# Unread products of constants in TensorE's waits: a two-layer attention and mixture-of-experts kernel

## The reference, cut to what matters

```
x = x + attn0(layernorm(x), ctx)   # 16 heads of 16, in windows of 128 queries and 128 keys
x = x + moe0(layernorm(x))         # 16 experts, top 2 (sigmoid gates), and a shared expert of 512
x = x + attn1(layernorm(x), ctx)   # 16 heads; 256 tokens share 256 keys
x = x + moe1(layernorm(x))         # 8 experts of 1024, top 2 (softmax gates), with biases
```

## Time and profile before

| | |
|---|---|
| median of three runs | 954.8 us (952.94 to 958.06) |
| the profiled execution | 952.44 us |
| its span, first to last instruction | 950.5 us |
| TensorE busy | 793.5 us, 83% |
| VectorE, ScalarE, GpSimd busy | 610.0, 382.6, 235.5 us |
| mean granted TensorE clock | 0.904 of 2.4 GHz |

### The profile page before, as it was taken

The page is one execution under the profiler, slowest core; times in us unless marked ns, Lnnn a source line. Parts: engine busy times, 40 slices in busy tenths (PEclk is TensorE's granted clock), DMA queues, the critical chain, the costliest instruction groups (busy, mean ns, idle before and its releaser), DMA issues.

```text
span 950.5 us, 23219 instructions
## 1 busy us (share of the span) xinstructions
PE 793.5 (83%) x8478; PEld 596.2 (63%) x8479; DVE 610.0 (64%) x1397; ACT 382.6 (40%) x750; POOL 235.5 (25%) x203
## 2 busy tenths in 40 slices
PE   5988997897897999987869999874029999999993
PEld 3545564654556888864525666563019999999992
DVE  3546777466745766759565888676975665556561
ACT  3425556342322322222324556655324444444440
POOL 1100000100014777742100000020033544444431
PEclk9986999798999999998976999875559999999996
DMA  9966402244324333339625320167332333333334
GB/s 267 103 75 92 140 7 68 89 133 133 102 65 143 103 99 105 99 114 186 74 38 75 71 91 3 46 231 284 110 122 47 72 71 71 73 67 67 72 65 111
DMA packets 72973, 94.66 MB, mean 100 GB/s; under 512 B 14320, under 2 KB 58224, under 8 KB 72880
## 3 DMA queue, kind: packets, MB, share of 16 engines
q1 hardware_dynamic: 57088, 62.17, 27.6%
q0 software_dynamic: 13872, 29.24, 12.4%
q10 hardware_dynamic: 1952, 2.39, 0.7%
HBM read 63.09 MB, written 19.92 MB: 87 GB/s over the span
## 4 chain that ended last, share of the span: by engine, by line
PE 60%; DVE 16%; issue 6%; DMA 4%; ACT 3%; POOL 1%; POOLq 0%; DVEq 0%; SPq 0%; ACTq 0%
PE bank L879 16%; PE bank L892 13%; PE bank L672 5%; PE bank L693 4%; PE bank L798 3%; DVE arena L1606 3%; PE bank L641 3%; PE bank L864 2%; PE bank L749 2%; DVE neg_max L1316 2%; PE bank L659 2%; PE bank L787 2%; PE bank L790 2%; PE bank L687 1%; DMA sum_d<-arena,put_i 1%
## 5 line engine op out<-in xcount | busy, mean ns | idle before, releaser
L879 PE MATMUL bank<-arena 128*128 128x128 f16 x3024 | 303.8, 221 | 14.5 <-DVE arena L1611 12.5
L892 PE MATMUL bank<-arena 128*128 x1224 | 282.9, 275 | 4.7 <-DVE arena L1619 2.9
L879 PEld LDWEIGHTS bank<-arena 128*128 x3024 | 264.7, 99 | 31.5 <-issue 15.4
L1760 POOL DMA_INDIRECT arena<-xn_d,get_i x87 | 92.1, 1059 | 210.7 <-DVE arena L1606 100.1
L1184 ACT ACTIVATE arena<-bank,arena 128x128 f32<-128x128 f32 x312 | 86.4, 376 | 125.7 <-DMA arena<-in_exp_b 67.3
L1316 DVE TENSOR_REDUCE neg_max<-bank 128x2 f32<-128x512 f32 (+1 forms) x180 | 117.3, 684 | 28.7 <-PE bank L641 27.8
L892 PEld LDWEIGHTS bank<-arena 128*128 128x128 f16 x1224 | 120.2, 98 | 15.9 <-issue 13.1
L1056 ACT ACTIVATE arena<-bank 128x1024 f32<-128x1024 f32 x96 | 96.5, 1026 | 15.4 <-PE bank L659 15.0
L1770 POOL DMA_INDIRECT sum_d<-arena,put_i x39 | 63.3, 1622 | 111.9 <-DVE arena L1632 101.5
L1619 DVE TENSOR_TENSOR arena<-arena 128x512 f16<-128x512 f32 (+1 forms) x126 | 74.7, 593 | 4.3
L1744 POOL DMA_DIRECT2D xn_d<-arena x8 | 6.7, 840 | 276.4 <-DVE arena L1385 276.4
(11 more groups left out here) (185 smaller groups left out, 1129.4 us busy)
## 6 DMA issues: line engine op xcount, KB each, us to landing
arena<-arena SPq DMA_DIRECT2D x96, 128.0 KB, 5.2
arena<-in_exp_up SPq DMA_DIRECT2D x16, 512.0 KB, 3.7
arena<-in_exp_dn SPq DMA_DIRECT2D x6, 1024.0 KB, 6.4
arena<-in_exp_up SPq DMA_DIRECT2D x5, 1024.0 KB, 6.0
arena<-in_exp_b SPq DMA_DIRECT2D x39, 128.0 KB, 3.0
arena<-in_ctxT SPq DMA_DIRECT2D x8, 512.0 KB, 7.2
arena<-in_exp_dn SPq DMA_DIRECT2D x16, 256.0 KB, 4.0
xn_d<-arena POOLq DMA_DIRECT2D x8, 512.0 KB, 5.8
```

What stands on the lines that cost most here:

```text
L879: last = mm(upP[u][:, m // (UB // 2), m % (UB // 2) * P:(m % (UB // 2) + 1) * P], weights(e, 0, w, k * UPW[l] + m * P, P), rowsT[u][x][:, ...
L892: last = mm(yP[u], hidT[u][x][:, k], weights(e, 1, w, k * D, D), start=n == 0, stop=n == n_second - 1)
L1760: pool.indirect_dma_start(rows[i % 2], None, xn_d[l], bass.IndirectOffsetOnAxis(ap=get_i[:, i:i + 1], axis=0)).then_inc(s["rows_in"][i % 2 ...
```

## The change

A helper `keep_running(to, n, cols)` multiplies the identity with the first `cols` columns of `consts`, n times, in float32, into a stretch of PSUM that nobody reads. It is called in TensorE's program alone; no other engine's program changes. Four of its places also get a wait of their own, so that the PSUM stretch is free. The diff (context cut):

```
+        spare = bank[:, 4]
...
+            def keep_running(to, n, cols):
+
+                for _ in range(n):
+                    mm(to[:, 0:cols], ident, consts[:, 0:cols], start=True, stop=True)
...
                 def turn_tokens(c, u):
+                    if l == 0 and c == NC - 1:
+                        pe.wait_ge(s["xT_ready"], c)
+                        keep_running(trT[:, 0], 3, 3 * P)
                     pe.wait_ge(s["xn_ready"], c + 1)
...  first_maxima:
                 for m in range(lo, hi):
+                    if l and m >= 2:
+                        if m == 2:
+                            pe.wait_ge(s["v_ready"], NC)
+                        keep_running(spare, 5 if m == 2 else 1, 3 * P if m == 2 else P)
                     after(pe, s["max_read"], m - 1)
...  turn_first:
+                if l:
+                    keep_running(spare, 2, P)
                 pe.wait_ge(s["max_read"], 4 * KV[l])
...  attend, maxima:
                     for m in range(lo, hi):
+                        if isinstance(i, int) and i == 1:
+                            if l == 0 and m == 0:
+                                pe.wait_ge(s["v_ready"], NC)
+                            if l == 0 and m == 2:
+                                keep_running(spare, 5, 3 * P)
+                            elif m:
+                                keep_running(spare, 1, P)
                         after(pe, s["max_read"], i * NM + m - 1)
...  attend, step:
                             maxima(i + 2, SPREAD[l][p], SPREAD[l][p + 1])
+                        if p == 0 and isinstance(i, int) and 13 <= i < 13 + (1 if l else FIRST0):
+                            keep_running(spare, 2, 2 * P)
                         if p == 0 and not first:
                             turn_back(i - 1)
...  route:
                 def score(c, u):
+                    if l:
+                        keep_running(bank[:, 2], 2, 2 * P)
                     pe.wait_ge(s["xT_ready"], NC + c + 1)
...  invert:
+                if l:
+                    pe.wait_ge(s["routed"], 3)
+                    keep_running(bank[:, 2], 13, 3 * P)
                 pe.wait_ge(s["routed"], 4)
...
                 if l:
+                    keep_running(bank[:, 2], 6, 3 * P)
                     pe.wait_ge(s["routed"], 6)
...  experts:
+                if l:
+                    pe.wait_ge(s["w_lo"], PIECES - 1)
+                    keep_running(bank[:, 0], 4, 3 * P)
                 pe.wait_ge(s["w_lo"], PIECES)
                 may_multiply(0)
```

## The result

The changed kernel takes 951.88 us (median of 20 runs, 944.8 to 956.03), the kernel before, run beside it, 957.51 us (20 runs, 948.52 to 962.95). The ratio is 0.9943, with a 95% interval of 0.992 to 0.9967: faster by 5.6 us, where 12.8 were forecast (954.8 to 942). The direction is right and the size is not; the time lies just outside the range of 934 to 951. Of the 9.9 us between forecast and result, 2.7 belong to the kernel before, whose median was 954.8 us over the three runs shown and is 957.5 over twenty; the gain is 5.6 us for 12.8 all the same.

The account below looks back on a forecast made before the run. It took TensorE's granted clock to set much of the time, where the others wait for TensorE. Terms summed to -11.5 us: 940.9 on the profiled execution's scale, 942 us after adding half of 2.4; range 934 to 951.

Parts of the forecast that it names:

- T1: End of layer 0's projections: three products hidden in a 2.27 us wait hold the clock; -1.7 us (bounds 0 and -1.9).
- T4: Late attention steps: two products hold the clock in layer 1's step 13, -2.8 us; layer 0's two such places 0.
- T3: Layer 1's first attention steps: +0.25 us if the clock is lost, -6.7 if held; taken as -0.7.
- I add half: Last adjustment: the shown runs' median is 2.4 us above the profiled execution; half added for clock luck, 940.9 to 942 us.
- T2: Layer 0's first attention steps: five hidden products, but the clock falls in the unfilled second wait; -0.3 us (-3.2 if held).
- rival A: Clock holds through both attentions' second waits, so their first steps gain more: 933 us, chance 0.12.
- T5: Layer 1's route: products ahead of each chunk's scores hold the clock, half the time with a fall; -5 us (bounds -6.7, +1.2).
- Rival B: Clock falls in layer 1's route as before, since 8-column scores and transposes do not hold it: 948 us, chance 0.16.
- T6: Ahead of the placing's products in layer 1: 13 products (about 11 us) and six (3.9 us) stay hidden; 0 us.
- Rival D: Slower: unread products run at half clock and outlast their waits, at the placing above all; 962 us, chance 0.05.
- T7: Layer 1's first expert products: four products bring the clock back earlier; -1.0 us (bounds +0.7 and -1.4).

Follow-up runs that it names:

- attn_only: Kernel before plus only the unread products where both attentions begin (blocks of five, singles, two ahead of the transposed maxima): 985.56 us, ratio 1.0008.
- route_only: Kernel before plus only the two unread products ahead of each chunk's scores in layer 1's route: 979.16 us, ratio 0.9929.
- tr_route: Kernel before plus eight float32 transposes of the identity ahead of each chunk's scores in layer 1's route: 979.22 us, a single execution.
- second_wait: no_single plus three float32 products of 384 columns inside step 0 of both layers: 970.2 us, ratio 0.9838.
- held: f16_single plus float16 products of 384 columns inside step 0 of both layers (four, then seven): 965.28 us, ratio 0.9833.
- no_single: Changed kernel without the single products between the maxima, blocks of five kept: 967.96 us, ratio 0.9827; run again 975.87 us, ratio 0.9872.
- f16_single: Changed kernel with each single float32 product between the maxima replaced by one float16 product of 512 columns: 974.63 us, ratio 0.9917.
- no_attn: Changed kernel without any unread products where the attentions begin, the others kept: 976.57 us, ratio 0.9929.
- before_again: Kernel before, unchanged, run for a second profile: 990.21 us, mean clock 0.898.

## Why the prediction was right or wrong

**The failed steps: what each term is measured against, and the price of a single product.** The terms were differences to one execution, in which the clock fell at every place that has a term. Such falls are not in every execution. Step 13 of layer 1 took 9.2 us without any product in attn_only and route_only, and 10.7 in tr_route; the end of layer 0's projections was 12.6 us without products in route_only and tr_route (which are the kernel before up to the route), and 14.2 or 14.3 in the other three. On the mean over the five profiles without products, T1 is -1.0 and not -1.7, and T4 -1.4 and not -2.8: 2.1 us of the sum of 11.5. T3, below, had a price wrong and is +0.5 for -0.7: 1.2 more. On the other side, the route's products hold the clock throughout in five of ten profiles that have them (15.7 us); in two it fell and came back (16.9), in three it fell and stayed (20.1, 20.4 and 20.3 us).

The runs on record say the same of the clock without a profile. In 63 executions of the kernel before, in the three groups, the mean clock lies between 0.896 and 0.918, 0.907 on the average, and an execution with 0.001 more is about 0.6 us shorter. The profiled one had 0.904, which is 2 us of lost clock above the ordinary. It was 5 us below the median of its 20 runs all the same (952.44 for 957.51), and that of the changed kernel 3 below its own. "I add half" made the forecast gain 12.8 against the median, 1.3 more than the sum; no run shows a reason for it.

**T1**, right in its mechanism: the three products took 2.10 us at 45.86, the real ones followed with 0.33 to spare, PEclk was 1.00. -1.7 in this profile.

**T2**, right against rival A, +0.4 for -0.3 in size. The clock fell at 72.7 (73 to 76 was said) and stayed low to 86.3. That the unfilled second wait is the reason was an argument; second_wait and held show it: with products in it, and nothing else new in layer 0 against no_single and f16_single, its steps 0 and 1 take 10.5 and 10.3 us for 13.6 to 14.0.

**T3**, wrong. "The single products between the maxima fit beside VectorE's 0.67 us per reduction" rested on a price by columns, from a run of 256-column products that follow each other. Between float16 groups a 128-column float32 product moves the next group by 0.42 or 0.72 us. At full clock that still fits (attn_only, 18.8 us); at half clock it does not, and the sum had no term for the clock falling while the maxima were still under way. It had: in the changed kernel's three profiles it fell 11.9, 6.0 and 6.5 us ahead of the first mark, and so ahead of the second wait to which the prediction gave its fall. The prediction had worked out 0.43 + 0.43 at half clock and called it 0.2 too much for each of 13; it did not put this into the sum, and it is 0.57 too much (0.54 and 0.72 for 0.69). Whether the two weight loads or something else of a float32 product make it so long was not separated. The start came 4.8, 2.9 and 3.1 us late in the three profiles. Without the single products it is 17.8 and 18.0, with float16 ones 18.9 and, at full clock throughout, 17.5. What was gained in return, a mean of 3.1 us in steps 0 and 1, is a matter of when the clock comes back. The term is +1.3 in the profile and about +0.5 on the mean, for -0.7.

**T4**, right: no slow stretch in step 13, 9.17 us from mark to mark for 12.02 (606.37 to 615.54). Its size on the mean is above.

**T5**, right: -6.6 in the profile, where -5 was taken for chance losses. Over all profiles with these products the stretch is 17.3 us on the mean for 23.0, and their 0.9 us ahead of the first scores is paid: -4.8. Rival B is out as the rule, since 8-column scores with transposes and 0.86 us of products hold the clock in most profiles, and by tr_route so do transposes in place of products but for 3.5 us. The chance given to a fall within the route was right: it came in five of ten, though in three of them the clock did not come back within the route.

**T6**, right: the 13 products took 10.27 us ("about 11") and the six 4.95, each with its real products still waiting for VectorE. Rival D is out (by its own terms, 955.1 + 7.7, it was 963 us and not 962).

**T7**, right: -0.7 in this profile, -1.3 on the mean, for -1.0.

**The sum.** The terms' means are -1.0, +0.3, +0.5, -1.4, -4.8, 0 and -1.3, and layer 0's late steps, counted at 0, give -0.8 (their clock falls now and then without products): about -8.5. By the three ratios (0.9943, 0.9924, 0.9952) it was -5.5, -7.5 and -4.7 us, each 2.3 to 3.4 either way. So 1 to 4 us are left, about what the intervals and means over few profiles allow. Part of it can be a clock that falls elsewhere when it is held here. From 165 to 315 us, layer 0's route and the start of its experts, where nothing is added, PEclk is 0.93, 0.89, 0.90 and 0.92 in the four profiles whose layer 0 is the kernel before's, and 0.89 in eight, 0.90 in one of the nine that have the change's products at layer 0's late steps. That is about 6 us more at half clock on the mean and at most 3 us of time (an estimate from these rows); with four profiles on one side it is not shown. route_only and no_attn have the same ratio, 0.9929, although the latter has T1, T4 and T7 as well, which should be worth 3.7 us: that would fit it, and the intervals do not exclude chance.

**The bound of a page.** The Trainium skill, "TensorE: Matmul & The Clock Gate", Part 1, puts the clock's warm-up below 1% of a typical kernel. The prediction took this for a bound on all that the clock can cost, and the sentence does not say so much: it is about the first warm-up. held takes 1.67% off [1.30, 2.04] by unread products alone, with a mean clock of 0.946 to 0.952 for 0.896 to 0.917 in its group, since here the clock is lost again and again at waits.

**What the change was worth, part by part.** The route's products make about all of it (route_only 0.9929); those where the attentions begin make nothing as they stand (attn_only 1.0008, no_attn 0.9929). They become worth some 10 us (0.9833 for 0.9929) when the single ones are float16 and the second wait is filled as well (held). Float16 alone does not show it (0.9917), and the filled wait without single products gave 0.9838 in its group for 0.9872 without it.

## What to carry to other kernels

A run of unread products is worth its place only if it reaches, without a second wait behind it, to the work that is bound by TensorE; look for the next wait after the one you fill. Price a filler by the start of the next instruction in the mix in which it stands, and at half clock, since it has to fit there too; between float16 products a float16 filler moved the next group by less (0.32 for 0.42 us at full clock, with four times the columns). Size a gain of clock by several profiles of the kernel before: where the clock falls is partly chance, and a single profile shows the falls of one execution.

## What the runs showed of the hardware

- A float32 product of 128 columns between float16 ones moves the next group by 0.42 us at 2.4 GHz and 0.72 at 1.2 (488.65 to 489.07, 495.85 to 496.57 in the profile after); a float16 product of 512 columns by 0.32 (512.29 to 512.61 in held).
- Float32 transposes help to hold the clock in layer 1's route: 16.9 us for 23.2, with 3.5 us at half clock (tr_route, one execution).
- The same code gets another clock from execution to execution: a mean of 0.896 to 0.918 in 63 executions of the kernel before.
- The same kernel took 957.5 us in the pair and 983 to 986 on the chips of the three groups, both with a full clock in layer 0's experts, whose loop took 119.4 and 148.5 us in the two profiles. The group where VectorE waits there, of the kernel before in its first profile and in before_again (300 to 440 us):

```profile
L1626 DVE TENSOR_SCALAR arena<-bank 128x256 f32<-128x256 f32 x47 | 19.9, 424 | 31.3 <-PE bank L892 28.6 <-issue 2.6
```

```profile
L1626 DVE TENSOR_SCALAR arena<-bank 128x256 f32<-128x256 f32 x40 | 16.8, 420 | 53.5 <-remote 52.0 <-PE bank L892 1.5
```

VectorE waits there for a release that the profile puts down to something outside its engines, not for TensorE. The row stands behind writes of ranked rows to memory; that they are slower in the groups is a guess, and whether it is the chip or something else is open.
